# Mixture-of-experts stages: down products with the gated values as weights, and the scatter-adds of a whole tile one after the other

## What is computed

```
idx   = the cap best-scored tokens of each expert            # 32 x 160
w     = the token's share for this expert (0 if not routed)
xe    = xf[idx]                                              # gather rows
up    = einsum('eci,eji->ecj', xe, w_up)                     # 256 -> 2 x 512
hact  = silu(gate half) * value half
ye    = einsum('ecj,eoj->eco', hact, w_down)                 # 512 -> 256
out   = zeros((T, C)).at[idx].add(w * ye)                    # scatter-add
# adapters: one of 16 per pair of experts, 256 -> 2 x 128 -> 256, times 0.05,
# with the same w; done here on the same gathered rows
```

## Time and profile before

| what | us or share |
| --- | --- |
| median of three runs | 1789.94 |
| profiled execution, first to last instruction | 1787.2 |
| stage `moe1e`, first up product to last add issued | 801.01 to 1124.19 |
| stage `moe2e`, first up product to last add issued | 1459.41 to 1781.54 |
| PE busy over the span | 1488.8 (83%) |
| POOL busy over the span | 564.3 (32%) |
| DMA engines, both kinds of queue, share of the span | 31.8% and 11.4% |

### The profile page before, as it was taken

How to read it: one execution, slowest core, us unless ns; L and a number is a source line. 1 busy time by engine, 2 the same in 40 slices (tenths; PEclk the granted TensorE clock), 3 DMA queues, 4 the chain that set the end, 5 groups by cost and what they waited for, 6 DMA issues and landing times. The chain is left out here.

```text
span 1787.2 us, 27066 instructions
## 1 busy us (share of the span) xinstructions
PE 1488.8 (83%) x9512; PEld 1127.3 (63%) x9512; DVE 977.1 (55%) x2816; ACT 728.9 (41%) x1775; POOL 564.3 (32%) x467
## 2 busy tenths in 40 slices
PE   6899989999999678339999997489995459999994
PEld 5566544555554454229889997255553349899994
DVE  8865677787873597855531111356566855521110
ACT  5222147666667375415423232114333425322331
POOL 6522210000000442321636455221211231636535
PEclk9989889999999898559999999699997569999997
DMA  3034363333300022325969894401112326879974
GB/s 104 18 127 129 107 131 63 79 55 79 55 26 1 12 95 83 150 44 174 246 194 258 245 246 65 133 25 35 48 36 95 118 71 201 225 221 247 265 193 47
DMA packets 113493, 212.11 MB, mean 119 GB/s; under 512 B 20085, under 2 KB 79386, under 8 KB 104154
## 3 DMA queue, kind: packets, MB, share of 16 engines
q1 hardware_dynamic: 87066, 178.93, 31.8%
q0 software_dynamic: 26304, 31.60, 11.4%
HBM read 158.71 MB, written 51.38 MB: 118 GB/s over the span
## 5 line engine op out<-in xcount | busy, mean ns | idle before, releaser
L952 DVE TENSOR_REDUCE attnm_top<-psum 128x1 f32<-128x384 f32 (+3 forms) x384 | 212.8, 597 | 56.4 <-PE psum L1037 52.3
L1174 ACT ACTIVATE attnm_prob<-psum 128x512 f32<-128x512 f32 (+1 forms) x384 | 192.1, 530 | 87.6 <-PE psum L1047 81.0
L2328 POOL DMA_INDIRECT x_sum<-moe1e_y,moe_scatter_i x76 | 119.7, 1575 | 128.2 <-ACT moe1e_y L2462 71.0
L2507 DVE SCALAR_TENSOR_TENSOR moe1e_h<-moe1e_gate,psum 128x160 f32<-128x160 f32 x160 | 50.6, 321 | 199.4 <-ACT moe1e_gate L2436 199.1
L2328 POOL DMA_INDIRECT out<-moe2e_y,moe_scatter_i x76 | 119.2, 1568 | 127.7 <-ACT moe2e_y L2462 70.5
L2507 DVE SCALAR_TENSOR_TENSOR moe2e_h<-moe2e_gate,psum 128x160 f32<-128x160 f32 x160 | 50.4, 321 | 198.8 <-ACT moe2e_gate L2436 198.6
L2383 PE MATMUL psum<-moe1e_xgT,moe_w_up 128*128 128x160 f32 x1024 | 152.2, 304 | 2.4 <-ACT moe1e_xgT L2452 2.4
L2383 PE MATMUL psum<-moe2e_xgT,moe_w_up 128*128 128x160 f32 x1024 | 150.7, 302 | 2.4 <-ACT moe2e_xgT L2452 2.4
L2383 PEld LDWEIGHTS psum<-moe1e_xgT,moe_w_up 128*128 128x128 f32 x1024 | 144.2, 193 | 4.8 <-issue 4.8
L2383 PEld LDWEIGHTS psum<-moe2e_xgT,moe_w_up 128*128 128x128 f32 x1024 | 142.7, 192 | 4.8 <-issue 4.8
L1348 POOL DMA_INDIRECT moe_xg<-xn_rows,moe_gather_i x80 | 84.3, 1054 | 159.3 <-DVE moe_gather_i L1536 93.0
(11 more groups left out here) (414 smaller groups left out, 3230.5 us busy)
## 6 DMA issues: line engine op xcount, KB each, us to landing
moe_w_up<-in_expert_up SPq DMA_DIRECT2D x64, 1024.0 KB, 7.5
moe_w_down<-in_expert_down SPq DMA_DIRECT2D x64, 512.0 KB, 3.5
attnm_q_hat<-q_parts SPq DMA_DIRECT2D x72, 128.0 KB, 4.4
moe_a_up<-in_adapter_up SPq DMA_DIRECT2D x32, 256.0 KB, 4.2
q_parts<-attnf_q_part SPq DMA_DIRECT2D x12, 512.0 KB, 2.8
attnm_k_hat<-k_parts SPq DMA_DIRECT2D x72, 64.0 KB, 2.3
x_res<-in_x SPq DMA_DIRECT2D x8, 512.0 KB, 9.4
v_tails<-attnf_v_tail SPq DMA_DIRECT2D x4, 1024.0 KB, 4.3
```

The costliest lines, as they stand in the source:

```text
L952: nc.vector.tensor_reduce(top[:, n // QUADS % 2, tiles[0]:tiles[-1] + 1, hh:hh + 1], s.ps[:, u.bank, 0:len(tiles) * width].rearrange("p (t ...
L1174: nc.scalar.activation(prob[:, i % NPROB, at:GROUP], s.ps[:, u.bank, at:GROUP], ACT.Exp).then_inc(taken[u.bank], 1)
L2328: nc.gpsimd.indirect_dma_start(total, bass.IndirectOffsetOnAxis(ap=rows, axis=0), y[:, q, k, :], None, bounds_check=TOKENS + SPARE - 1, oo ...
L2507: nc.vector.scalar_tensor_tensor(out=h[:, n % 2, i, :], in0=gate[:, i, :], scalar=1.0 if i < INTER // P else SCALE_A, in1=s.ps[:, u.bank, ...
```

## The change

- **Down product**: `h` (128 slots) is the stationary operand and `w_down` (256 columns) moves, 5 matmuls per expert, so the result comes out with slots on partitions. `copy_down`, `turn_y`, `weigh_y` and `yT` are gone; ACT weighs straight from PSUM bank 5 (`weigh`, L2502).
- **Tails**: the last 32 slots of the four experts of a quad are computed together (`tails`, L2442): 20 matmuls with 32 weight columns and 256 moving columns, each expert on its own 32 output partitions. For it all of a quad's `h` and `w_down` must be kept to the quad's end (`h` grows from 2 to 5 buffers, `HELD`).
- **Loads**: `w_down` and `a_down` of the next quad are issued only after the last down product of the quad, in one go, with two `w_up` among them. `w_up` and `a_up` go as before.
- **Adds**: one expert's tile has no token twice, so it is added whole with `whole`, now made for both halves of the experts; tile 4 is added twice as before. That makes six adds a quad, and each waits until the one before has landed (`landed`), by a single semaphore `y_out`. In the last quad tile 3 and tile 4 are added by first and second picks.
- **Gather order**: tiles 0 and 4 first, then 1 and 2, then 3 (`FETCH`); the first expert's up products wait for the first two alone, and the other transposes come between them.

```
-TWO = [(0, 1), (2, 3), (4,)]
-ALONE = TWO[0]
+FETCH = [(0, 4), (1, 2), (3,)]
+TAIL = EQ
...
-        if self.half:
-            spare_no = ...
-            chain.link(... self.of_any ...)
-            nc.vector.scalar_tensor_tensor(out=self.whole[:], ...)
+        (the same without the if)
...
+    HELD = [0, 1, 2, 3, 4, 0, 1, 2]
+    h = sb("h", [P, EQ + 1, PAIRS, CAP])
...
+            ORDER += [("x", 0, 0)]
+            for i in range(PAIRS):
+                ORDER += [("up", 0, i)]
+                if i in (1, 3):
+                    ORDER += [("x", 0, (i + 1) // 2)]
         if n == 1:
+            ORDER += [("x", 1, i) for i in range(len(FETCH))]
         if n + 1 < 2 * EQ:
+            ORDER += [("up", n + 1, i) for i in range(PAIRS)]
+        if n % EQ == EQ - 1:
+            ORDER += [("tails", n // EQ, None)]
         ORDER += [("down", n, None)]
...
+            for q in range(2):
+                if last and q == 1:
+                    break
+                first = 0 if q == 0 else EQ + 2
+                for n in range(first, EQ * q + EQ):
+                    next_up(n)
+                sp.wait_ge(full[u_down[EQ * q + EQ - 1].bank], down[q])
+                for k in range(EQ):
+                    m.load_down(sp, t * 2 * EQ + EQ * q + EQ + k, k)
+                    if k % 2 == 0:
+                        m.load_a_down(sp, t * EQ + (q + 1) * EQ // 2 + k // 2, k // 2)
+                    if q == 0 and k % 2:
+                        next_up(EQ + k // 2)
...
+            done = add.done
+            landed(done)
+            if quad > 0:
                 pool.sem_inc(y_free[1 - q], 1)
+            for k in range(EQ - 1):
+                landed(done)
+                done = store(k, whole[k])
+            landed(done)
+            if quad < QUADS_E - 1:
+                done = store(EQ - 1, whole[EQ - 1])
+                landed(done)
+                done = store(TAIL, first[TAIL])
+                landed(done)
+                done = store(TAIL, second[TAIL])
+            else:
+                store(TAIL, first[TAIL])
+                done = store(EQ - 1, first[EQ - 1])
+                landed(done)
+                store(TAIL, second[TAIL])
+                done = store(EQ - 1, second[EQ - 1])
+            add.done = done
...
+            for i in range(PAIRS):
+                pe.wait_ge(taken[u_up[n, i].bank], u_up[n, i].after(t))
+                ins = nc.tensor.matmul(s.ps[:, u.bank, 0:C], h[:, HELD[n], i, 0:P], down_weight(k, i),
+                                       start=(i == 0), stop=(i == PAIRS - 1))
...
+        def tails(t, q):
+            for i in range(PAIRS):
+                for k in range(EQ):
+                    rows = slice((CAP - P) * k, (CAP - P) * (k + 1))
+                    ins = nc.tensor.matmul(s.ps[rows, u.bank, 0:C], h[:, HELD[EQ * q + k], i, P:CAP], down_weight(k, i),
+                                           start=(i == 0), stop=(i == PAIRS - 1), skip_group_check=True)
```

More of the change, by code:

```diff
@@ L1344, in gather @@
         q = quad % 2
-        for i, tiles in enumerate(TWO):
+        for i, tiles in enumerate(FETCH):
             for k in tiles:
@@ L2244, in experts @@
             u_down[n] = banks.use(5)
-        else:
-            for j in range(len(TWO)) if what == "x" else (i,):
-                (u_x if what == "x" else u_y)[n, j] = banks.use(6 + ring % 2)
-                ring += 1
+        elif what == "x":
+            u_x[n, i] = banks.use(6 + ring % 2)
+            ring += 1
+        else:
+            u_tails[n] = banks.use(6 + ring % 2)
+            ring += 1
+    X_OF = [next(i for i, tiles in enumerate(FETCH) if k in tiles) for k in range(EQ)]
     late = m.choices[1]
@@ L2308, in gather @@
             m.gather(pool, quad)
+        stored = itertools.count(1)
         def add(quad):
             q, t = quad % 2, quad // 2
+            choice, at = m.choices[quad // late.quads], quad % late.quads
+            whole = [choice.whole[:, at, k:k + 1] for k in range(EQ)]
             first, second = ([scatter_i[:, (quad * 2 + i) * ST_TILES + k:(quad * 2 + i) * ST_TILES + k + 1]
                               for k in range(ST_TILES)] for i in range(2))
-            phases = [list(enumerate(first)), list(enumerate(second))]
@@ L2317, in add, with store @@
-            if quad == QUADS_E - 1:
-                phases = [[(k, late.whole[:, late.quads - 1, k:k + 1])] for k in ALONE] + [of[len(ALONE):] for of in phases]
+            def store(k, rows):
+                u = u_tails[q] if k == TAIL else u_down[EQ * q + k]
+                pool.wait_ge(taken[u.bank], u.after(t))
+                nc.gpsimd.indirect_dma_start(total, bass.IndirectOffsetOnAxis(ap=rows, axis=0),
+                                             y[:, q, k, :], None, bounds_check=TOKENS + SPARE - 1, oob_is_err=True,
+                                             compute_op=ALU.add).then_inc(y_out, 16)
+                return next(stored)
@@ L2319, in add, with landed @@
+            def landed(n):
+                if n > 0:
+                    pool.wait_ge(y_out, 16 * n)
+            done = add.done
+            landed(done)
             if quad > 0:
-                pool.wait_ge(y_out[1 - q], 16 * ST_TILES * 2 * ((quad - 1) // 2 + 1))
                 pool.sem_inc(y_free[1 - q], 1)
[L2322 to L2329, removed]
-                                                 compute_op=ALU.add).then_inc(y_out[q], 16)
-                    done += 1
+            for k in range(EQ - 1):
+                landed(done)
+                done = store(k, whole[k])
@@ L2457, in weigh_y, with weigh @@
+            ins.then_inc(taken[u.bank], 1)
+        def weigh(t, q, tile):
+            u = u_tails[q] if tile == TAIL else u_down[EQ * q + tile]
             act.wait_ge(full[u.bank], u.after(t))
[L2458 removed]
+            if tile == 0:
                 act.wait_ge(y_free[q], t + 1)
                 act.wait_ge(weighed, 2 * t + q + 1)
[L2461 to L2463 removed]
@@ L2464, in weigh_y @@
-            ins.then_inc(taken[u.bank], 1)
+            nc.scalar.activation(y[:, q, tile, :], s.ps[:, u.bank, 0:C], ACT.Copy,
+                                 scale=weight[:, q, tile:tile + 1]).then_inc(taken[u.bank], 1)
         def choose(step, k):
```

164 lines of the change are left out of this document (69 added, 95 removed).

## The result

The change makes the kernel slower. In four runs beside four of the kernel before it took 1827.38 us (1821.90 to 1836.39) against 1789.63 (1783.09 to 1791.12): a ratio of 1.022, 95% interval 1.019 to 1.025, or 37.8 us. The forecast was 1784, its range ended at 1815. The profiled execution after has a span of 1834.5 us against 1787.2, 47.3 more.

A forecast was written before the change was run, and what follows sets the result against it. POOL's chain of serial adds was taken to bound the second half of each expert stage. Both stages change by 42 x 5.7 - 244.6 = -5.2 us: profiled span 1787.2 to 1782, median about 1784 us, range 1748 to 1815.

The forecast's parts named there:

- The bound: Second half of each expert stage: POOL no longer catches up and hides PE's gain; 37 us a quad, PE's 34.7.
- 83.7 + 21 L: POOL's us from quad 4's gather to the last add issue; L: one add's issue to the next's, waiting for it.
- quad 6's surplus: In POOL's sum, quad 6 was forecast at six waits of 4.9 us, 29.4 us, as the loads run out.
- L = 5.7: Forecast us from one add's issue to the next waiting add's issue on POOL, while weights are loaded.
- Rival 2: Bursts of weight loads hold POOL's adds up: slower, +12 from L = 6.1, +28 (1818 us) at 6.5; chance 0.19.
- Rival 1: POOL's adds land quickly, L below 5.3: faster, -35 (1755 us) at L = 5.0; chance 0.24.
- PE's part: PE's products, turns and waits in the expert stages: -4.6 us a turn, and -3.0 at a stage's start.
- Rival 3: PE's tails don't run side by side: 8.7 us a quad, both stages +31, 1821 us; chance 0.05.
- 9.3 shorter: Quad 4's gather begins 9.3 us earlier: -3.0 start, -4.6 turn 0, -1.65 three down products of turn 1.
- +37: Upper bound of POOL's sum over both stages, at L = 6.7: 1827 us.

The follow-up runs named there:

- two rounds: Changed kernel with the adds of the kernel before: five first picks, one wait, five second picks a quad; 1751.88 us (0.980), again 1767.14 us (0.989).

## Why the prediction was wrong

**The bound: right.** POOL's chain of adds ends the stages, as the prediction said it would. Its sum, 83.7 + 21 L from the gather of quad 4 to the last add, holds: with the measured L and quad 6's surplus (6 x 0.37 and 6 x 0.39) it gives 228.1 and 225.7; the windows show 227.8 and 225.8. It holds without loads too (83.7 + 21 x 4.56 + 6 x 0.8 = 184.3 against 184.3 and 184.2), where one distance in quad 6 was 10.8 us, since the tile's own product came late (ACT had weighed it by 1704.8, and the add began at 1706.35). After the change the last down product ends at 1800.23, 28.6 us before the last add, where the prediction looked for 20 or more. Since L is measured on the same rows, this shows that nothing else is in the stretch; what L would be is the part that had to be foreseen.

**The step that failed: L = 5.7.** It is 6.7, and 21 x 2 x 1.0 = 42 us of the 47 that the second halves exceed the forecast's by; the other 5 are quad 6, taken at 4.9 "as the loads run out", where one more bunch made the first distance 8.4 and 8.2. The prediction got 5.7 by taking the median landing of the adds before, 5.0, plus 0.8, and a little off because an add alone has no four others before it.

The 5.0 rests on half of the adds. In that stretch the trace has a landing for 30 of the 60 only, all of quads 1, 3 and 5; their mean is 5.1, so it wasn't the median that misled. The other quads show themselves in POOL's own waits: from the last issue of a first round to the first of the second, quads 2 to 5 took 6.44, 4.46, 8.97 and 4.45 us in `moe1e` and 6.10, 4.36, 8.04 and 4.73 in `moe2e`, a mean of 5.94. The long ones are in the even quads, which the median didn't have. Quad 4 of `moe1e`, before:

```profile
1012.73 1.55 POOL L2328 DMA_INDIRECT x_sum<-moe1e_y,moe_scatter_i  x1 [0.31 <-issue]
1021.70 1.55 POOL L2328 DMA_INDIRECT x_sum<-moe1e_y,moe_scatter_i  x1 [7.41 <-DMA x_sum<-moe1e_y,moe_scatter_i]
```

And being alone gave nothing. In the kernel before, with serial adds and the same order of loads, L is 6.19 and 6.56, 6.37 in the mean, and the landings of quads 2 to 5 of `moe1e`, all 24 on record, have a lowest, median and highest of

```profile
DMA to landing us min/median/max: 3.6/5.5/9.8
```

So of the 1.0 us some 0.2 is the sample and the discount, 0.4 came with the adds standing alone (against only eight waits before; why they take longer no run shows), and the last 0.3 to 0.5 with the bunch. The upper bound, 6.7, from the worst stretch of the earlier trace rows, came out near the measured mean, though it was the median of one quad's adds in rounds.

**Rival 2 was half of it.** It named the bunch, L = 6.5 and 1818 us. The bunch is real: first distances of 10 us behind it, and 0.5 us of L and about 20 us when it is spread. But with its loads spread the kernel is still slower than before by 19.5 us, and the old kernel, which has no bunch of eight, loses 39 by the serial adds alone. The weight loads lengthen a lone add in every order that was run, and each wait pays for it. Its evidence against, "the total taken is less than before", was true of the share (0.60 of the engines against 0.78 in the second halves) and no comfort: by the windows' GB/s the bytes of a second half hardly fell, from 39.5 to 38.3 MB, and they were spread over a stretch 30 us longer.

**Rival 1** would have needed L below 5.3, and with two thirds of the loads' bytes left L is still 5.45 and 6.05. The quoted rule of the Trainium skill (page "DMA: Bandwidth & Descriptors", section "Anatomy of one DMA — SWDGE (gpsimd) path") gave, as an estimate, L = 4.6. The run without loads agrees with 4.56; under the loads of the change L is 6.7.

**PE's part: right where it can be seen.** Rival 3 fell: the chain of waits after shows the 40 tail instructions and the down product:

```profile
1544.18 2.16 PE psum L2428 x10
...
1546.68 2.30 PE psum L2442 x40
```

2.16 us (forecast 2.17) and 2.30 (2.6). The first up product comes 7.05 us after the first gather of `moe1e`, before 10.81: -3.8, where -3.0 was forecast. The first half was to become 9.3 shorter. With two rounds it did: 127.28 and 126.25 us, -10.0 and -9.6. With the change's serial adds it is -7.3 and only -2.3: 9.0 us short of the forecast in sum, which the prediction had no term for. In the second of these PE is busy 120.6 us, with two rounds 117.6 for the same 897 instructions, so 3.0 of the 7.3 between them are instructions at a lower clock (0.94 against 0.96) or drawn out; the rest are waits. The serial adds alone don't make them, since with the loads spread the first halves are -10.0 and -8.3. With no loads at all they take 129.57 and 129.41 us, so the bunch isn't all of it either, and the cause stays open.

**The sum.** Forecast -5.2 from span to span, measured +47.3. The 52.5 between them are +47 in the second halves, +9 in the first ones and -3.4 from what is outside the stages. The chances put 0.31 on slower, and the mechanism that the prediction's own bound priced at +37 got 0.19 with its range ended at L = 6.45.

## What to carry to other kernels

Before four DMAs are traded for four waits on landings, price the wait under the traffic that will be there: here one more add in a round costs POOL 1.86 us, and an add that is waited for 4.5 quiet and 6.7 under weight loads. A chain of 21 waits turns 1 us of error into 21, so look at what its price rests on: how many of the transfers have a landing on record, which they are, and what the engine's own waits say of the others. Sum with the mean; after the change the medians of the distances lie 0.3 and 0.7 us below it. Where two edits come together, ask what each does by itself: here everything but the serial adds is worth 1 to 2%, and the serial adds cost 2.1% in the kernel before and 3.4 to 4.3% in the new one, against its two measurements with rounds.

## What was not expected of the hardware

- A 128 KB add issued between 0.5 us before and 3.2 us after the last of eight weight loads was followed by the next one only 9.9 to 10.9 us later (4 cases), against 4.6 quiet. Four loads of 1.9 MB in the kernel before did as much: 10.8 and 10.5 us.
- The granted clock is lower where PE waits more: 0.88 in the second halves after, where PE is busy 174 of 227 us, 0.96 with two rounds, where it is busy 167 of 188. Around the 5.8 us wait that ends at 1654.42 it was 1.00 before (2.4 GHz), 0.50 in the 4.6 us behind it (1.2 GHz, PE busy 2.67 us), 0.65 in the next 6.5 and 1.00 again from 1665.5. The same 1210 PE instructions took 7 us more of busy time; POOL's chain hid that.
- Two measurements of one kernel (two rounds) on two occasions gave 1751.9 and 1767.1 us with the kernel before at 1788.2 and 1787.9, so a ratio to the kernel before doesn't carry over from one job to another to better than about 1% (0.980 and 0.989).
